# A pooled-embedding recommendation kernel on one core: counting matmuls in runs of three units instead of two, samples dealt in twelves, and a prologue in another order

## The reference, cut to what matters

```
x      = mlp(dense_x, bot)                                            # 13 -> 512 -> 256 -> 64, ReLU
pooled = vmap(lambda tab, ix: take(tab, ix, axis=0).sum(axis=1))      # 26 x 2048 x 64
Tcat   = concat([x[:, None, :], transpose(pooled, (1, 0, 2))], axis=1)   # 27 vectors a sample
Z      = einsum('bim,bjm->bij', Tcat, Tcat)                           # pairwise products, lower triangle
out    = mlp(concat([x, Z[:, li, lj]]), top)                          # 415 -> 512 -> 256 -> 1, sigmoid
```

## Time and profile before

| what | value |
|---|---|
| median of 3 runs | 2857.62 us (2854.86 to 2863.55) |
| the profiled execution | 2854.84 us, of which the span on the core is 2853.0 us |
| PE busy | 2743.9 us, 96% |
| ACT busy | 2112.7 us, 74% |
| DVE busy | 1994.1 us, 70% |
| POOL busy | 1809.4 us, 63% |
| sums (L693) | 8232 matmuls, 2019.2 us |
| counts (L674) | 14448 matmuls, 521.6 us |
| unpacks (L837) | 1848, 1710.5 us |

### The profile page before, as it was taken

One profiled execution on the slowest core, in us unless ns is written; L12 is line 12 of the kernel. 1 busy time (PEld: TensorE's weight loads), 2 busy tenths in 40 slices (PEclk: granted clock), 3 DMA queues, 4 the chain that ended last, 5 costly groups with the idle time before them and its releaser, 6 DMA issues.

```text
span 2853.0 us, 65593 instructions
## 1 busy us (share of the span) xinstructions
PE 2743.9 (96%) x24204; PEld 1305.1 (46%) x24204; DVE 1994.1 (70%) x3358; ACT 2112.7 (74%) x2496; POOL 1809.4 (63%) x1640
## 2 busy tenths in 40 slices
PE   5999999999999999999999999999999999999998
PEld 2344444444444444444444444444444444447963
DVE  4477787777877778787787877878778787753420
ACT  2778878788787887878878788787887878872431
POOL 3277777777777777777777777777777777400000
PEclk8999999999999999999999999999999999997579
DMA  2112122121221212212122121221212212007830
GB/s 69 62 32 76 28 78 75 32 76 28 78 75 32 76 29 78 74 32 77 31 76 74 32 77 30 76 74 32 77 30 77 74 32 74 20 26 111 137 85 0
DMA packets 173102, 167.99 MB, mean 59 GB/s; under 512 B 116104, under 2 KB 134328, under 8 KB 167476
## 3 DMA queue, kind: packets, MB, share of 16 engines
q1 hardware_dynamic: 121380, 110.94, 13.9%
q0 software_dynamic: 51200, 52.53, 9.4%
q10 hardware_dynamic: 272, 0.52, 0.1%
HBM read 143.83 MB, written 20.05 MB: 57 GB/s over the span
## 4 chain that ended last, share of the span: by engine, by line
PE 81%; ACT 11%; issue 3%; SPq 2%; DMA 1%; DVE 1%; ACTq 1%; DVEq 0%; POOL 0%; POOLq 0%
PE ps L693 58%; PE ps L674 14%; ACT counts L837 6%; PE ps L637 5%; ACT parts L799 3%; PE ps L764 3%; SPq L509 1%; ACT parts L806 1%; SPq L516 0%; ACT h_bot L850 0%; ACT pooled_sb L828 0%; SPq L532 0%; ACTq L834 0%; DMA pooled<-pooled_sb 0%; DMA look_in<-in_r_indices 0%
## 5 line engine op out<-in xcount | busy, mean ns | idle before, releaser
L611 POOL DMA_INDIRECT rows<-in_L_rec_tables,look x1600 | 1790.1, 1119 | 613.9 <-issue 453.7
L837 ACT CAST counts<-ps 128x792 int32<-128x792 f32 (+1 forms) x1848 | 1710.5, 983 | 471.7 <-PE ps L674 460.9
L693 PE MATMUL ps<-counts,parts 128*128 128x512 fp8e3 x8232 | 2019.2, 389 | 0.0
L693 PEld LDWEIGHTS ps<-counts,parts 128*128 128x128 f16 x8232 | 718.0, 96 | 912.1 <-issue 6.0
L1053 DVE TENSOR_TENSOR onehot_p<-iota_by_unit,place 128x1024 bf16<-128x1024 bf16 x924 | 637.4, 690 | 391.2 <-PE ps L674 363.2
L674 PEld LDWEIGHTS ps<-onehot_c,onehot_p 60*128 60x128 bf16 x14448 | 369.6, 95 | 479.9 <-ACT counts L837 272.2
L674 PE MATMUL ps<-onehot_c,onehot_p 60*128 60x99 bf16 x14448 | 521.6, 208 | 56.4 <-ACT counts L837 23.9
L1058 DVE TENSOR_TENSOR onehot_c<-column_c,weighted_s 128x792 bf16<-128x792 bf16 x924 | 520.4, 563 | 0.0
L1014 DVE SCALAR_TENSOR_TENSOR raw<-raw,coef_next,parts 128x896 f32<-128x896 f32 x147 | 168.8, 1148 | 60.0 <-ACT parts L799 59.9
L1087 DVE TENSOR_REDUCE rows<-rows 128x64 f32<-128x384 f32 (+1 forms) x240 | 189.7, 790 | 13.9 <-DVE pooled_sb L1064 13.9
L1064 DVE SCALAR_TENSOR_TENSOR pooled_sb<-ps,coef,pooled_sb 64x512 f32<-64x512 f32 x84 | 61.9, 737 | 145.8 <-ACT pooled_sb L828 145.8
(11 more groups left out here) (82 smaller groups left out, 524.8 us busy)
## 6 DMA issues: line engine op xcount, KB each, us to landing
raw<-in_L_rec_tables SPq DMA_DIRECT2D x21, 1792.0 KB
raw<-in_L_rec_tables SPq DMA_DIRECT2D x21, 1344.0 KB
rows<-in_L_rec_tables,look POOLq DMA_INDIRECT x1600
pooled<-pooled_sb SPq DMA_DIRECT2D x84, 128.0 KB, 2.3
slots<-pooled SPq DMA_DIRECT2D x30, 352.0 KB, 8.0
products<-zt SPq DMA_DIRECT2D x16, 351.0 KB
idx_raw<-in_r_indices SPq DMA_DIRECT2D x42, 79.7 KB
gathered<-bags_t SPq DMA_DIRECT2D x42, 64.0 KB
```

The costliest lines, as they stand in the source:

```text
L611: nc.gpsimd.indirect_dma_start(rows[:, s, l, :], None, rows_flat, bass.IndirectOffsetOnAxis(ap=look[:, c, s * PL + l:s * PL + l + 1].bitca ...
L693: mm = nc.tensor.matmul(acc[k % 2][:, 0:NB], parts[:, j, :], count_bytes[k % 2][:, j % COLS, 0:NB, j // COLS], start=(j == 0), stop=(j == ...
L837: nc.scalar.copy(counts[k % 2][:, :, u * UG * GS:(u * UG + g) * GS].rearrange("p c (g h s) -> p h g c s", h=HALVES, s=HS), unit_ps[unit_bu ...
```

## The change

Three things are changed.

1. `phase` goes by three units: count 3 units (24 matmuls), then 12 sums; seven times, then the last unit and 14 sums. The turns of the bags and the indices stand ahead of unit 9 instead of unit 10. The three PSUM buffers, the two buffers of pairs and everything that ACT and DVE do between units and pairs stay as they were.
2. Samples are dealt to units in another way, so that the samples of a unit's half lie side by side: a counting matmul writes its 33 x 3 results into PSUM with a distance of 12 between the runs of 3, and the unpack writes runs of 12 int32 where it wrote runs of 3. The last unit holds 8 samples in 3 groups of one half, computed with 6 matmuls; the index blocks are padded to 88 groups, and the indices of a table are loaded by ten transfers instead of three.
3. The prologue: SP issues four weight loads and the lookups first and without waiting; ACT's queue issues the three biases; ACT copies the turned weights out, four at a time, where DVE copied them one by one; PE turns the indices after the weights.

```diff
+    US = UG * GS
+    UH = UG * HS
+    UNITS = -(-NB // US)
+    WHOLE = (UNITS - 1) * UG
+    LAST = NB - (UNITS - 1) * US
+    LAST_GROUPS = -(-LAST // HS)
+    GROUPS = WHOLE + LAST_GROUPS
+    GPAD = UNITS * UG
...
                 for h in range(HALVES):
-                    sp.dma_start(idx_raw[0:GROUPS - 1, :, h * HP:h * HP + HK],
-                                 flat[:, 0:cut].rearrange("k (g h r) -> h g k r", h=HALVES, r=HK)[h]
-                                 ).then_inc(idx_loaded, 16)
+                    for x in range(UG):
+                        sp.dma_start(idx_raw[x:WHOLE:UG, :, h * HP:h * HP + HK],
+                                     flat[:, 0:cut].rearrange("k (u h x r) -> h x u k r", h=HALVES, x=UG, r=HK)[h, x]
+                                     ).then_inc(idx_loaded, 16)
...
-            sp.wait_ge(const_step, 4)
-            load_indices(0)
             with nc.allow_non_contiguous_dma(reason="small weights and biases"):
-                for dst, src in weight_loads:
+                for dst, src in weight_loads[:4]:
                     sp.dma_start(dst, src).then_inc(weights_in, 16)
+                load_lookups(0)
+                sp.wait_ge(const_step, 4)
+                load_indices(0)
...
-                        last = nc.tensor.matmul(unit_ps[unit_buffer(k, u)][:, h, x * HC:(x + 1) * HC],
+                        last = nc.tensor.matmul(unit_ps[unit_buffer(k, u)][:, h, :].rearrange(
+                            "p (c x s) -> p x c s", x=UG, s=HS)[:, x, :, :],
...
-                for u in range(0, UNITS, 2):
-                    if bags and u == 10:
+                for u in range(0, UNITS, 3):
+                    if bags and u == 9:
                         turn_bags(t, GB * t)
-                    if indices and u == 10:
+                    if indices and u == 9:
                         turn_indices(t + 1)
-                    j1 = SPAN if u == UNITS - 2 else PER_UNIT * (u + 2)
+                    end = min(u + 3, UNITS)
+                    j1 = SPAN if end == UNITS else PER_UNIT * end
                     await_rows(t, k, PER_UNIT * u, j1)
-                    count_unit(tn, kn, u)
-                    count_unit(tn, kn, u + 1)
-                    for j in range(PER_UNIT * u, PER_UNIT * (u + 2)):
+                    for v in range(u, end):
+                        count_unit(tn, kn, v)
+                    for j in range(PER_UNIT * u, PER_UNIT * end):
                         sum_rows(t, k, j)
...
             pe.wait_ge(consts_ready, 1)
-            turn_indices(0, first=True)
             pe.wait_ge(weights_in, 16 * len(weight_loads))
             turn(pe, turns, turned, unturned)
+            turn_indices(0, first=True)
...
-                g = len(units_of(u))
+                halves = HALVES if u < UNITS - 1 else 1
                 nc.scalar.copy(
-                    counts[k % 2][:, :, u * UG * GS:(u * UG + g) * GS].rearrange(
-                        "p c (g h s) -> p h g c s", h=HALVES, s=HS),
-                    unit_ps[unit_buffer(k, u)][:, :, 0:g * HC].rearrange("p h (g c s) -> p h g c s", c=COLS, s=HS),
+                    counts[k % 2][:, :, u * US:u * US + halves * UH].rearrange("p c (h b) -> p h c b", b=UH),
+                    unit_ps[unit_buffer(k, u)][:, 0:halves, :].rearrange("p h (c b) -> p h c b", b=UH),
                 ).then_inc(counts_ready, 1)
...
+            for i, dst in enumerate(unturned_groups):
+                act.wait_ge(turned, i + 1)
+                m, items, kp = dst.shape
+                nc.scalar.copy(dst, banks[i % 4][0:m, 0:items * P].rearrange("p (k c) -> p k c", c=P)[:, :, 0:kp]
+                               ).then_inc(unturned, 1)
             convert_indices(0)
...
-            unturn(dve, turns, turned, unturned)
```

More of the change, by code:

```diff
@@ L66, in build @@
     BLOCKS = B // NB
-    GROUPS = -(-NB // GS)
-    TAIL = NB - (GROUPS - 1) * GS
     UG = 4
+    US = UG * GS
[5 more added lines that the diff above has]
+    GROUPS = WHOLE + LAST_GROUPS
+    TAIL = LAST - (LAST_GROUPS - 1) * HS
+    GPAD = UNITS * UG
+    assert LAST <= UH
     LG = 2
     SUBS = UG // LG
-    UNITS = -(-GROUPS // UG)
     PAIRS = UNITS // 2
-    BPAD = GROUPS * GS
+    BPAD = (UNITS - 1) * US + UH
     CHUNKS = 7
@@ L187, in build @@
         b_top2c = sb(ctx, "b_top2c", [1, 1], F32)
-        idx_raw = sb(ctx, "idx_raw", [GROUPS, BLOCKS, P], I32)
+        idx_raw = sb(ctx, "idx_raw", [GPAD, BLOCKS, P], I32)
         idx_f = idx_raw[:, :, :].bitcast(F32)
@@ L222, in build @@
         weighted_s = sb(loop, "weighted_s", [P, UNITS * SUBS, HS, LG], BF16)
-        NI = BLOCKS * GROUPS
+        NI = BLOCKS * GPAD
         idx_t = sb(loop, "idx_t", [P, NI], F32)
         scratch = sb(loop, "scratch", [P, NI], F32)
-        NIP = NI + UNITS * UG - GROUPS
+        NIP = NI
         place_next = sb(loop, "place_next", [P, 3, NIP], BF16)
@@ L646, in turn_indices @@
                 for k in range(BLOCKS):
-                    last = nc.tensor.transpose(into[:, k * GROUPS:(k + 1) * GROUPS], idx_f[:, k, :],
-                                               ident[0:GROUPS, 0:GROUPS])
+                    last = nc.tensor.transpose(into[:, k * GPAD:(k + 1) * GPAD], idx_f[:, k, :],
+                                               ident[0:GPAD, 0:GPAD])
                 last.then_inc(idx_turned, 1)
@@ L809, in convert_indices @@
             def convert_indices(t):
-                act.wait_ge(idx_loaded, 48 * t + 48)
-                nc.scalar.copy(idx_f[:, :, 0:TAIL * L], idx_raw[:, :, 0:TAIL * L]).then_inc(idx_converted, 1)
-                for cols in (slice(TAIL * L, HK), slice(HP, HP + HK)):
-                    nc.scalar.copy(idx_f[0:GROUPS - 1, :, cols], idx_raw[0:GROUPS - 1, :, cols]
-                                   ).then_inc(idx_converted, 1)
+                act.wait_ge(idx_loaded, 160 * t + 160)
+                nc.scalar.copy(idx_f[0:GROUPS, :, 0:TAIL * L], idx_raw[0:GROUPS, :, 0:TAIL * L]).then_inc(idx_converted, 1)
+                for groups, cols in ((GROUPS - 1, slice(TAIL * L, HK)), (WHOLE, slice(HP, HP + HK))):
+                    nc.scalar.copy(idx_f[0:groups, :, cols], idx_raw[0:groups, :, cols]).then_inc(idx_converted, 1)
             def copy_bags(n):
@@ L834, in unpack_unit @@
                 act.wait_ge(unit_counted, HALVES * n + HALVES)
-                g = len(units_of(u))
+                halves = HALVES if u < UNITS - 1 else 1
                 nc.scalar.copy(
-                    counts[k % 2][:, :, u * UG * GS:(u * UG + g) * GS].rearrange(
-                        "p c (g h s) -> p h g c s", h=HALVES, s=HS),
-                    unit_ps[unit_buffer(k, u)][:, :, 0:g * HC].rearrange("p h (g c s) -> p h g c s", c=COLS, s=HS),
+                    counts[k % 2][:, :, u * US:u * US + halves * UH].rearrange("p c (h b) -> p h c b", b=UH),
+                    unit_ps[unit_buffer(k, u)][:, 0:halves, :].rearrange("p h (c b) -> p h c b", b=UH),
                 ).then_inc(counts_ready, 1)
+            with nc.allow_non_contiguous_dma(reason="biases"):
+                for dst, src in weight_loads[4:]:
+                    act.dma_start(dst, src).then_inc(weights_in, 16)
+            unturned_groups = [xT[:, i * 4 * P:(i + 1) * 4 * P].rearrange("p (k c) -> p k c", c=P)
+                               for i in range(B // P // 4)]
+            unturned_groups.append(w_bot0T[:, :].rearrange("p (k c) -> p k c", c=P))
+            unturned_groups += [w_bot1T[:, :, m * P:(m + 1) * P] for m in range(NBOT[2] // P)]
+            unturned_groups.append(w_bot2T[:, :, :])
+            for i, dst in enumerate(unturned_groups):
[3 more added lines that the diff above has]
+                               ).then_inc(unturned, 1)
             convert_indices(0)
@@ L1049, in onehot_pair @@
                 whole = [P, 2 * SUBS, P, LG]
-                g0 = k * GROUPS + 2 * UG * d
+                g0 = k * GPAD + 2 * UG * d
                 at = place[:, 0, g0:g0 + 2 * UG].rearrange("p (u a g) -> p u a g", a=1, g=LG).to_broadcast(whole)
```

10 lines of the change are left out of this document (6 added, 4 removed).

## The result

The changed kernel takes 2971.03 us (2968.24 to 2971.94, 4 runs) against 2856.91 for the kernel before on the same chip (4 runs): ratio 1.0402, 95% interval 1.0389 to 1.0414. The forecast was 2926. The profiled execution has a span of 2968.4 us, 115.4 more than before; the mean granted clock is 0.960, and 0.965 before.

What follows compares the result with a forecast made beforehand. PE's own list was taken to bound phases 1 and 2, with waits and a busy ACT in phases 0 and 3. Per table +4.1 us, 20 times 82; 2854.8 + 82 - 14 = 2923 profiled, 2926 median; range 2862 to 2990.

Steps and rivals of the forecast that it cites:

- rival 2: Runs of three in PSUM make a counting matmul a third slower, 0.016 each, 60 us: 2986; chance 0.15.
- DVE's windows: Only 1.04 us fits between two pairs in groups of three; units 8, 14, 20 late by 0.55, 1.14, 1.20 in phase 1.
- unpack: ACT's unpack of 792 elements, writing runs of 12, takes 0.77 us instead of 0.87; bounds 0.74 and 0.87.
- pair 2: Phase 0: PE can use this DVE pair 6.76 us after the first count, a wait of 3.1 us.
- prologue: Weights first and no DVE copies: bottom layers start at 19.4 instead of 33.63, 14 us less; bounds 9 and 17.
- strided output: I take nothing: Counting matmuls writing runs of three to PSUM cost nothing extra, since 99 and 512 columns both take near 0.45 ns a column.
- the terms for ACT and DVE: Phase 3: ACT decides from unit 9 on, DVE's wait at pair 7 lies inside; 29.86 against 29.54, 0.32 more.

Runs made afterwards that it cites:

- DVE's new order: Changed kernel with pair 2 ahead of pool_bags and adopt_coef, and pool_bags, pieces, chunks and index copy moved to windows with room: 2883.09 us, ratio 1.0103.
- the kernel of 2787.69 us: Changed kernel with DVE's work reordered, counting matmuls writing contiguously, and 32 transposes (64 instructions) ahead of PE's loop: 2787.69 us, ratio 0.9768.
- 2974.38 us: Changed kernel with only 32 transposes added ahead of PE's loop, so its head lies 64 instructions later: 2974.38 us, ratio 1.042.
- 2845.76: Changed kernel with DVE's work reordered and 32 transposes (64 instructions) ahead of PE's loop, strided writes kept: 2845.76 us, ratio 0.9969.

## Why the prediction was right in its sign and 45 us short

2971 us lies inside the range of 2862 to 2990, but outside the 2905 to 2950 that belonged to the forecast by itself, and nearer to rival 2 (2986) than to 2926. What happened is the forecast's waits with rival 2's slower counts, and two further terms that nearly cancel.

**Right: DVE's windows.** 0.55, 1.14 and 1.20 us late were forecast, in groups whose counts take 0.68. They take 0.81, so PE comes later and the waits are 0.36, 0.93 and 0.96 [the gaps between sums in phase 1, 1.49, 2.06 and 2.09 against 1.13]. With contiguous writes the waits are those of the forecast to 0.02 us, phase 1 is 31.13, forecast 31.15, and phase 2 28.50, forecast 28.50. Moving DVE's work took them away without taking any off DVE.

**Right, or near: unpack, pair 2, prologue.** 2.26 for three unpacks, the last about 0.84, is 0.71 each: forecast 0.77, and under the lower bound of 0.74. With the gap gone pair 2 serves PE 6.69 after the first count, forecast 6.76. The first layer starts at 20.05 and the first sum at 102.5, forecast 19.4 and 102. With the three index transfers of before, the same prologue is worth 20 us, 16.7 of them ahead of the first sum.

**Wrong: "strided output: I take nothing".** The nearness of 99 columns and 512 at 0.45 ns a column showed what a column costs, not what a write in pieces costs. It is 0.011 a pair, 23%, where rival 2 had 0.016. 87 pairs make 0.95 us a phase; in phases 1 and 3 the waits gave 0.6 to 0.7 of it back (31.44 against 31.13, 33.00 against 32.73), as that rival says. It is worth 45 us in the changed kernel, 73 with groups of two (2882.33 to 2809.25), and 61 with DVE's new order (2883.09 to 2822.02). The Trainium skill (PSUM — Partial Sum Buffer, Specifications (TRN2)) says that a pattern that isn't contiguous in PSUM slows matmuls significantly; here the runs agree for the write, 23%. So the rule that spoke against the change was true, and I gave it 0.15.

**Missed: the jump.** Phase 3 was forecast at 29.86 and is 33.00. In the last pass, which doesn't jump back, it is 30.3, and 29.87 with contiguous writes: the terms for ACT and DVE were right. My step cost the groups of PE's list and ACT's work, and no term for the loop's back edge. In the kernel before, 18 sums (4.16 us) and 8 more cover both gaps, but for 8.8 us. The changed kernel has 14 sums there (3.26), and then 24 counts, 48 instructions that PE is through with in 0.81 us. So both gaps lie open: 47.6 us. With groups of two in the changed kernel the two gaps cost 2.0 and 12.6 us in all.

**Missed: the clock behind a wait.** Phase 0 came out at 31.24 against 32.60, which looks like a term too large. It isn't: 2.5 us of the gap lie ahead of the first sum, in phase 3's account, and stand in place of most of the wait for pair 2. With the gap gone, phase 0 is 33.59, 1.0 over the forecast. Of that 0.6 is the low clock behind the wait for pair 2 (32.98 in the passes without it); the other 0.4 I put down to the wider counts, which isn't shown.

**The account**, each step the difference of two kernels that ran: the prologue -20 (2853.96 to 2833.94); units dealt in twelves with the faster unpack -25 (to 2809.25); strided writes +73 (to 2882.33); groups of three +89 (to 2971.03). Together 117, of which 3 lie between the runs of the kernel before in the two comparisons (2853.96 and 2856.91). The steps hold in this order only: with contiguous writes groups of three cost 117 (2809.25 to 2925.94), and the writes then 45.

**The sum.** Forecast a table +4.1, measured +6.46. In the kernel with contiguous writes the phases are 30.50, 31.13, 28.50 and 32.73, 122.86 against 122.11 forecast: there the gap (+2.9 in phase 3) and the cover it gives (-2.1 in phase 0) nearly cancel, and the 45 us that were short are those of the writes. That the forecast missed by just this one term is luck: two errors of opposite sign, each about as large as the writes' 2.3 us a table, stood beside it.

## What to carry to other kernels

When a group grows, list for each buffered hand-over which instruction releases it and which uses it: windows shrink by one group for every third pair here, and the work between can often be moved into the wide ones at no cost. Put long work of an engine, here 18 sums and not 14, across a loop's back edge, and look at waits put down to issue there; where a gap stands at the same instruction of each pass, shift the code and see. Let the reader of PSUM gather and the matmul write in a row; the other way round made each counting matmul 23% longer.

## What the runs showed of the hardware

- From the branch (1098.86) to the next instruction that PE's sequencer takes (1102.29) are 3.4 us in the changed kernel, and 1059.62 to 1063.04 before. Over the 19 jumps it is 3.4 to 3.9 us in both, 3.6 in the middle; the longest was 4.1, in the kernel of 2787.69 us.
- A second gap, 2.0 to 2.3 us, came after 21 matmuls of the loop, and went with a shift of 64 instructions and came back with one of 256.
- A matmul of 99 columns that writes 33 runs of 3 fp32 into PSUM at a distance of 12 takes 0.058 us a concurrent pair against 0.047.
- On ACT an unpack of 792 elements took 1001 ns writing runs of 3 int32 into SBUF and 825 ns writing runs of 12, whether it read runs of 12 or of 3.
- After a wait of 2.65 us the granted clock fell to 1.2 GHz in 15 of 20 passes (2974.38 us), and sums then start 0.427 apart. In the kernel before it fell in 4 passes, behind waits of 1.8 to 2.0 us, and not in others with waits as long. In the kernels of 2882.33, 2845.76 and 2809.25 us, whose longest waits in the loop are 1.6, 1.0 and 1.8 us, it didn't fall once; in that of 2787.69 us it fell once, in the first pass, behind a wait of 2.1.
- What stays open: why the branch takes 3.4 us, what the second gap waits for, and whether another alignment would also shorten the first gap; only shifts of 0, 64 and 256 instructions were tried.
